# A graph kernel: scatters held at two points of each slot, record codes stored as pairs, six source masks by ScalarE, and the third layer norm in six parts

## The reference

```python
edge_index = stack([src, dst])                       # 400000 edges, dst sorted
h = maximum(_layernorm(x), 0)                        # x is 12500 x 48
x = x + (segment_sum(edge_weight[:, None] * h[dst], src, N) @ weight + bias)
h = maximum(_layernorm(x), 0)
x = x + ((1 + eps[0]) * h + segment_sum(maximum(h[src] + edge_attr_48, 0), dst, N))
h = maximum(_layernorm(x), 0)
x = x + L2(h)     # twice: symmetric-normalised sum over the edges and self loops
h = maximum(_layernorm(x), 0)
x = x + L3(h)     # the same once, in the other direction
return x
```

## Time and profile before

| | us |
|---|---|
| runs | 10912.69, 10917.33, 10930.52 |
| median | 10917.33 |
| profiled execution, its own time | 10818.04 |
| its span | 10816.2 |
| busy: PE, DVE, ACT, POOL | 6417.2, 4776.5, 3992.4, 4088.1 |

### The profile page before, as it was taken

The page is one execution under the profiler, slowest core; times in us unless marked ns, Lnnn a source line. Parts: engine busy times, 40 slices in busy tenths (PEclk is TensorE's granted clock), DMA queues, the critical chain, the costliest instruction groups (busy, mean ns, idle before and its releaser), DMA issues.

```text
span 10816.2 us, 266700 instructions
## 1 busy us (share of the span) xinstructions
PE 6417.2 (59%) x100278; PEld 5569.8 (51%) x100279; DVE 4776.5 (44%) x7168; ACT 3992.4 (37%) x6938; POOL 4088.1 (38%) x4193
## 2 busy tenths in 40 slices
PE   5444444444444444444444444445999979999999
PEld 4333333333333333333333333335888879999998
DVE  5444444444444444444444443448999940111000
ACT  3333333333333333333333333335888820000333
POOL 2444444444444444444444444443888820000000
PEclk6666666666666666666666666667999989999999
DMA  6444444444444444444444444445999978888998
GB/s 172 141 146 146 143 143 140 142 138 146 144 144 146 147 144 142 139 137 142 145 146 147 147 142 138 145 148 180 317 317 317 316 247 265 275 279 273 195 204 178
DMA packets 1738803, 1964.50 MB, mean 182 GB/s; under 512 B 897469, under 2 KB 1403119, under 8 KB 1737791
## 3 DMA queue, kind: packets, MB, share of 16 engines
q1 hardware_dynamic: 1337520, 1347.06, 43.2%
q10 hardware_dynamic: 300646, 448.79, 12.1%
q0 software_dynamic: 100000, 158.60, 4.7%
HBM read 1258.29 MB, written 618.65 MB: 174 GB/s over the span
## 4 chain that ended last, share of the span: by engine, by line
PE 38%; another core or an unknown queue 25%; issue 13%; DVE 8%; ACT 8%; ACTq 3%; DMA 2%; POOL 1%; SPq 1%; DVEq 1%; POOLq 0%
PE pG L2174 7%; PE pT L2057 6%; ACT stg L2431 4%; PE pG L2013 3%; PE pT L2061 2%; PE pT L2174 2%; PE pG L2024 2%; PE pG L2226 2%; PE pR L2174 2%; PE pG L2022 2%; PE pG L2213 2%; DVE msum L1825 2%; ACT dfar L2398 1%; PE pG L2138 1%
## 5 line engine op out<-in xcount | busy, mean ns | idle before, releaser
L1359 POOL DMA_INDIRECT recB<-rec,qpos x3125 | 3046.9, 975 | 4294.4 <-issue 3403.0
L2057 PE MATMUL pT<-soh,doh 128*128 128x128 bf16 x10600 | 1771.6, 268 | 3412.7 <-ACT stg L2431 3032.7
L2431 ACT CAST stg<-pT 128x512 fp8e4<-128x512 f32 x2650 | 1499.7, 585 | 3989.4 <-remote 3050.9
L2057 PEld LDWEIGHTS pT<-soh,doh 128*128 128x128 bf16 x10600 | 1027.9, 117 | 3642.7 <-ACT stg L2431 3154.7
L1641 DVE TENSOR_TENSOR rec<-pG,wN 128x480 f32<-128x480 f32 x314 | 205.5, 654 | 2252.6 <-PE pG L2013 2241.9
L1628 DVE TENSOR_TENSOR soh<-smd,pG 128x1280 bf16<-128x1280 bf16 x530 | 432.5, 816 | 1314.4 <-remote 866.9
L2061 PE MATMUL pT<-car,qidb 128*128 128x256 fp8e4 x2597 | 925.1, 356 | 0.0
L2138 PE MATMUL pG<-mpl,doh 128*128 128x144 bf16 x10388 | 764.3, 227 | 34.0 <-POOL mpl L1380 25.0
L1628 DVE TENSOR_TENSOR doh<-dm,pG 128x2560 bf16<-128x2560 bf16 x530 | 782.7, 1477 | 1.5 <-ACT dm L2509 0.9
L1628 DVE TENSOR_TENSOR doh<-smd,pG 128x2560 bf16<-128x2560 bf16 x530 | 783.1, 1478 | 0.0
L2138 PEld LDWEIGHTS pG<-mpl,doh 128*128 128x128 bf16 x10388 | 666.0, 96 | 63.6 <-POOL mpl L1380 49.1
(11 more groups left out here) (266 smaller groups left out, 14329.2 us busy)
## 6 DMA issues: line engine op xcount, KB each, us to landing
recB<-zt ACTq DMA_DIRECT2D x102, 2425.5 KB
brec<-recB SPq DMA_DIRECT2D x477, 495.0 KB
erec<-recB SPq DMA_DIRECT2D x477, 495.0 KB, 5.5
cl<-cA SPq DMA_DIRECT2D x80, 2560.0 KB, 10.8
cA<-stg ACTq DMA_DIRECT2D x530, 320.0 KB
cl<-cA SPq DMA_DIRECT2D x40, 2720.0 KB, 11.1
drow<-dlD SPq DMA_DIRECT2D x157, 640.0 KB, 5.8
srowB<-srD SPq DMA_DIRECT2D x265, 320.0 KB, 5.8
```

The lines of the kernel that those rows point to most:

```text
L1359: p.indirect_dma_start(recF, bass.IndirectOffsetOnAxis(ap=qpos[:, s, c:c + 1], axis=0), rec[:, s, c, :], None).then_inc(s_sc[s], 16)
L2057: ins = t.matmul(bank[:, h * 256 + b * 128:h * 256 + b * 128 + 128], doh[:, o, 2 * e + b, h * 128:(h + 1) * 128], soh[:, o, 2 * e + b, :], ...
L2431: a.copy(stg[:, o, :, e * 256:(e + 1) * 256], B8[6 + (g * 5 + e) % 2][:, :].rearrange("p (h x) -> p h x", h=2), saturate=False).then_inc(e ...
```

## The change

Five things change.

1. In `scatter`, POOL waits ahead of the scatters 7 and 14 of each slot until `e_ca` has reached the count of `PACE`, from chunk 2 on. Chunk 1 is now written out ahead of the loop, without these waits. The counts start from the second group that the slot sums (`SUMMED[s][1]`), five to a group.
2. The two codes are written into the records as bfloat16 pairs (`meta`, and −1 in the empty records). `places` and `codes` go; DVE's `one_hots` reads the loaded records. The load of `brec` waits for ACT's evictions too.
3. In the third stage ACT makes the masks of six groups (`BY_ACT`), DVE those of four.
4. The layer norm between the stages goes in the six parts of `UN`. SP loads all of `part`, from 49 stored chunks on, its parts between the first loads of `cl`; PE waits for each part.
5. At the start, the first prefill is issued ahead of the table's zeros, and the large load of x after the second prefill.

A tenth check of the input's form joins the nine. The diff, cut to its core:

```diff
@@ -1245,9 +1262,13 @@
+        BY_ACT = [1, 3, 4, 6, 8, 9]
+        BY_DVE = [g for g in range(JG) if g not in BY_ACT]
@@ -1344,25 +1365,36 @@
-            def scatter(K, s, first=False):
+            PACE = {0: {7: 9, 14: 14}, 1: {7: 9, 14: 14}, 2: {7: 14, 14: 15}}
+
+            def paced(K, s, c):
+
+                back, g = SUMMED[s][1]
+                hold(p, e_ca, ((K - back) * JG + g) * 5 + PACE[s][c])
+
...
                 if first:
-                    p.wait_ge(q_ld[2], 64)
+                    p.wait_ge(s_p0, 32)
...
                 for c in range(15 if first else 0, SB):
+                    if pace and c in PACE[s]:
+                        paced(K, s, c)
                     p.indirect_dma_start(recF, bass.IndirectOffsetOnAxis(ap=qpos[:, s, c:c + 1], axis=0),
                                          rec[:, s, c, :], None).then_inc(s_sc[s], 16)
 
             scatter(0, 2, True)
-            with p.Fori(1, NK) as K:
+            for s in range(3):
+                scatter(1, s)
+            with p.Fori(2, NK) as K:
                 for s in range(3):
-                    scatter(K, s)
+                    scatter(K, s, pace=True)
@@ -1672,10 +1705,9 @@
-                v.wait_ge(e_sm, c + 1)
+                v.wait_ge(l_b[r], K * 64 + (g // 5 * 32 + 32))
                 reached(v, e_ca, c * 5 - 5)
-                one_hots(soh[:, o, :, :], smd[:, r, :, 0, :], GB, 128, ioA)
-                v.wait_ge(l_b[r], K * 64 + (g // 5 * 32 + 32))
+                one_hots(soh[:, o, :, :], brec_u[:, r, :, 97, :], GB, 128, ioA)
@@ -1683,7 +1715,7 @@
-                one_hots(doh[:, o, :, :], smd[:, r, :, 1, :], GB, 256, ioA)
+                one_hots(doh[:, o, :, :], brec_u[:, r, :, 98, :], GB, 256, ioA)
@@ -1794,16 +1826,16 @@
-                    if g % 2 == 0:
+                    if g in BY_DVE:
...
-                    v.wait_ge(m_dm, c + 1)
+                    v.wait_ge(k_e[r], K * 32 + (g // 5 * 16 + 16))
                     reached(v, m_sc, c - 4)
-                    one_hots(doh5[:, r, :, :], dm5[:, r, :, :], GB, 256, ioB).then_inc(m_do, 1)
+                    one_hots(doh5[:, r, :, :], erec_u[:, r, :, 98, :], GB, 256, ioB).then_inc(m_do, 1)
@@ -1828,17 +1860,52 @@
-                collect(NK - 1, (NK - 1) % 2)
-                nch.mark("free")
-                for b, (lo, hi) in enumerate(HALF):
-                    v.wait_ge(s_half[b], 32)
+
+                def centred(u):
...
-                    centre(2, b, qx3, qst)
-                summed(2, SQ2, hs_)
-                for b in range(2):
-                    scaled(2, b, SQ2, True)
-                    rests(2, b, xpc, qh3, qh_u, scr, scr_u)
+                    nch(v.tensor_reduce(qst[:, 0, lo:hi], qx3[:, lo:hi, :], AX.X, ALU.add))
...
+                centred(0)
+                collect(NK - 1, (NK - 1) % 2)
+                varied(0)
+                normed(0)
+                centred(1)
+                varied(1)
...
+                for u in range(2, len(UN)):
+                    varied(u)
+                    if u + 1 < len(UN):
+                        centred(u + 1)
+                    normed(u)
@@ -2154,6 +2221,7 @@
                 gather1(NK - 1, JG - 1, (NK - 1) % 2)
+                t.wait_ge(m_ev, NK)
...
-                                for b in ({0: 0, 2: 1}[u],) if u in (0, 2) else ():
-                                    t.wait_ge(e_qn, qn[f"pcs2{b}"])
-                                    t.wait_ge(t_sq, SQ2 + 6 + 2 * b)
+                                t.wait_ge(e_qn, qn[f"pcs2{u}"])
+                                t.wait_ge(t_sq, sqn[f"lo{u}"])
@@ -2386,8 +2453,10 @@
-                a.copy(rec[:, s, :, 97], srcl[:, bass.ds(ncol(K, s), SB)])
-                a.copy(rec[:, s, :, 98], dlK[:, bass.ds(ncol(K, s), SB)]).then_inc(e_me, 1)
+                a.copy(rec_u[:, s, :, 97, :],
+                       srcl[:, bass.ds(ncol(K, s), SB)].unsqueeze(2).to_broadcast([128, SB, 2]))
+                a.copy(rec_u[:, s, :, 98, :],
+                       dlK[:, bass.ds(ncol(K, s), SB)].unsqueeze(2).to_broadcast([128, SB, 2])).then_inc(e_me, 1)
@@ -2401,26 +2470,11 @@
-            def places(K, g):
-                c = K * JG + g
-                r = g % 5
-                a.wait_ge(l_b[r], K * 64 + (g // 5 * 32 + 32))
-                reached(a, e_pl, c - 4)
-                a.copy(smd[:, r, :, :, :],
-                       brec[:, r, :, 97:99].unsqueeze(3).to_broadcast([128, GB, 2, 2])).then_inc(e_sm, 1)
...
-                a.copy(smK[:, g * GB:(g + 1) * GB], smd[:, g % 5, :, 0, 0])
+                a.wait_ge(l_b[g % 5], K * 64 + (g // 5 * 32 + 32))
+                a.copy(smK[:, g * GB:(g + 1) * GB], brec_u[:, g % 5, :, 97, 1])
@@ -2501,25 +2554,18 @@
-                def codes(K, g):
-                    c = K * JG + g
-                    r = g % 5
-                    a.wait_ge(k_e[r], K * 32 + (g // 5 * 16 + 16))
-                    reached(a, m_do, c - 4)
-                    a.copy(dm5[:, r, :, :], erec[:, r, :, 98:99].to_broadcast([128, GB, 2])).then_inc(m_dm, 1)
-
@@ -2527,28 +2573,45 @@
-                    if not (known and K == NK - 1 and g >= JG - 2):
-                        codes(K + (g + 2) // JG, (g + 2) % JG)
...
-                    n = g + (2 if o else 3)
-                    if not (known and K == NK - 1 and n >= JG):
-                        (none_away if o else distances)(K + n // JG, n % JG)
...
+                    for n, part_ in ((g + 2, none_away), (g + 3, distances)):
+                        if n % JG in BY_ACT and not (known and K == NK - 1 and n >= JG):
+                            part_(K + n // JG, n % JG)
...
-                a.wait_ge(e_qn, qn["free"])
-                hold(a, s_nw, NK * 16)
-                for b, (lo, hi) in enumerate(HALF):
@@ -2597,13 +2660,12 @@
-            sp.dma_start(qx3[:, 8:NB - 1, :], x[8 * 128:(NB - 1) * 128, :].rearrange("(j p) d -> p j d", p=128)
-                         ).then_inc(q_ld[3], 16)
             sp.wait_ge(e_q, qm["c0"])
-            sp.dma_start(qx3[0:N - (NB - 1) * 128, NB - 1, :], x[(NB - 1) * 128:N, :]).then_inc(q_ld[3], 16)
             sp.dma_start(hT[NP:NPX, :].rearrange("(p r) c -> p (r c)", p=128),
                          zz[:, 0:144].bitcast(BF16)).then_inc(q_st, 16)
             sp.wait_ge(e_q, qm["zt"])
+            for h in range(2):
+                prefill(sp, 0, h, s_p0)
             sp.wait_ge(q_st, 32)
@@ -2635,6 +2697,7 @@
                 held(sp, e_ag, c - 4)
+                held(sp, e_cv, (c - 5) * 5 + 1)
@@ -2651,14 +2714,14 @@
-            sp.wait_ge(q_ld[2], 32)
-            for h in range(2):
-                prefill(sp, 0, h, q_ld[2])
             sp.wait_ge(e_q, qm["codes"])
             load_ea(0, 2)
+            sp.wait_ge(q_ld[0], 48)
             for h in range(2):
                 prefill(sp, 1, h)
-            sp.wait_ge(q_ld[0], 48)
+            sp.dma_start(qx3[:, 8:NB - 1, :], x[8 * 128:(NB - 1) * 128, :].rearrange("(j p) d -> p j d", p=128)
+                         ).then_inc(q_ld[3], 16)
+            sp.dma_start(qx3[0:N - (NB - 1) * 128, NB - 1, :], x[(NB - 1) * 128:N, :]).then_inc(q_ld[3], 16)
@@ -2713,10 +2775,10 @@
-                        hold(sp, *((m_sT, K * 5 + (g - 3) // 2) if g % 2 else (m_sU, K * 5 + (g - 4) // 2)))
-                    tab, w = (srD8, 64) if g % 2 else (srD, 128)
+                        hold(sp, *rowed(K - (g < 5), (g - 5) % JG))
+                    tab, w = (srD8, 64) if g in BY_ACT else (srD, 128)
@@ -2735,26 +2797,44 @@
-                steps(sp, step)
-                store_chunk(NK - 1)
-                sp.wait_ge(s_nw, NK * 16)
-                sp.wait_ge(e_qn, qn["free"])
-                for b, (lo, hi) in enumerate(HALF):
-                    sp.dma_start(qh3[:, lo:hi, :], part[lo * 128:hi * 128, :].rearrange("(j p) c -> p j c", p=128)
...
+                def load_part(u):
+
+                    lo, hi = UP[u]
+                    if u >= 2:
+                        hold(sp, s_half[u % 2], u // 2 * 32)
+                    sp.dma_start(qh3[:, lo:hi, :], part[lo * 128:hi * 128, :].rearrange("(j p) c -> p j c", p=128)
+                                 ).then_inc(s_half[u % 2], 16)
+                    sp.dma_start(scr[:, lo:hi, :], part[NPX + lo * 128:NPX + hi * 128, :].rearrange("(j p) c -> p j c", p=128)
+                                 ).then_inc(s_half[u % 2], 16)
+
+                steps(sp, step)
+                hold(sp, s_nw, KL * 16)
+                load_part(0)
+                load_cA(0, 0, (0,))
+                load_part(1)
+                hold(sp, m_ad, NK * JG)
+                load_cA(0, 0, (1,))
+                load_part(2)
+                store_chunk(NK - 1)
+                load_cA(0, 0, (2,))
+                load_part(3)
+                load_part(4)
+                hold(sp, s_nw, NK * 16)
+                load_part(5)
+                load_cA(0, 0, (3, 4, 5))
```

(32 more changed lines are left out.)

122 lines of the change are left out of this document (80 added, 42 removed).

## The result

The changed kernel took 10292.74 us (median of 4 runs, 10284.63 to 10311.25) against 10923.19 before; the ratio is 0.9426, with a 95% interval of 0.9409 to 0.9443. The range held the time, but the forecast (10710) did not: the kernel gained three times what I had said.

A forecast was written before the change was run, and what follows sets the result against it. First half bound by waits, third stage by DVE; −102 (waits) − 30 (codes) − 33 (third stage) − 40 (layer) = −205 of the profiled 10818.0, so 10613, by the median's 1.0092 10710 us; range 10200 to 10930, forecast's own 10584 to 10822.

The forecast's parts named there:

- What bounds the first half: First half: bound by waits; a burst of scatters holds back PE's signals, which clear some 3 us after it.
- The count of the waits that bind: POOL's scatters: slot 0 stops at 7 and 14, slot 1 at 14, slot 2 at 7; 4 waits a chunk.
- The price of a pause: First half: each binding wait costs 3.05 us less one step, 2.16 to 2.57 us; 8.6 to 10.3 a chunk.
- rival C: First half: a short burst clears sooner, in 1.07 us; 10291 us by the median, chance 0.17.
- What passes in the fresh runs: First half: 13.6 steps a chunk leave the free stretch; with the pauses' cost, −2.0 us a chunk, −102 us.
- Codes as pairs: First half: ACT's casts `smd` and `dm` go, so DVE's `soh` waits less; −30 us taken, at most 211.3.
- Third stage: Third stage: DVE makes one source mask fewer a chunk, −38 us; −33 taken because DMA is close.
- The bound named next: Third stage: DMA at 22.8 us a chunk stands next behind DVE at 23.0.
- The layer in parts: Between third and dense stage: PE waits for one part at a time; −40 us, bounds −20 and −49.
- Start: Start of the kernel: the x load leaves SP's queue ahead of `drow`; 0 us, bounds −15 and +10.
- Rivals D and E: First half: PE's clock stays low, 11293 us, chance 0.13; scatters wait for DVE's one-hots, 11015 us, chance 0.03.

The follow-up runs named there:

- before_paced: The kernel before with the two waits a slot alone, codes, third stage, layer and start unchanged; 10322.49 us, ratio 0.9471.
- act_five: The changed kernel with five source masks a chunk by ACT and five by DVE, as before the change; 10277.64 us, ratio 0.9434 to before.
- no_pace_act64: The changed kernel without its two waits a slot, with 64 one-element copies on ACT ahead of its chunk loop; 10949.0 us, ratio 1.0048 to before.

## Why the prediction was wrong

1. **What bounds the first half: right as far as the traces go.** Beside a burst PE's work passes in the first part of the run and comes back some 3 us behind the last scatter. That the burst itself holds its signals back is the reading that fits all eight kernels; no run shows the mechanism. The waits were the largest term, as forecast, and they alone give what the first half gained.

2. **The count of the waits that bind: wrong.** "Slot 1 at 14 alone, slot 2 at 7 alone, so 4 waits a chunk". The counts start from the second group of the slot, which the text on the change says; in slots 1 and 2 I took them from the first, five steps too low. In the trace of before the steps done from that base are 7.1, 6.2 and 7.0 at scatter 7 of the three slots and 8.4, 7.2 and 9.0 at scatter 14, all under the thresholds. Slot 1 stops at 7 too (7.0 us on the mean) and slot 2's pause at 7 is 13.8 us. Five waits bind.

3. **The price of a pause: right in size.** 4 × (3.05 less one step) was 8.6 to 10.3 us a chunk. The trace shows 10.5 more in the first 3 us behind the runs (19.5 against 9.0). That is for three more gaps of over 3 us (six, where before had three) and one of 1.7 us: five pauses came, but the gap ahead of slot 2 vanished and that ahead of slot 1 nearly did. Nor does a run of 7 clear as soon as rival C had it (1.07 us). PE begins 8.0 matmul records in the first 3 us behind such a run and 12.8 in the fourth, against 7.4 and 8.8 behind the bursts of 20 before. So the mechanism of C, whose time (10291) came out, is not what happened.

4. **What passes in the fresh runs, and what it is worth: the step that failed.** I gave "13.6 steps a chunk that leave the free stretch" at 0.74 to 0.89 us, 10 to 12 us, and took −2.0 a chunk for the waits. No step left it. Counted by evictions, as in the prediction, 17.4 steps a chunk began beside the scatters before the change and 9.3 after, so eight moved into the pauses and gaps. What moved the other way is the work that stands behind the steps in PE's program. A pause lets PE finish the slot's steps; next come the gathers for the following slot and, behind the first group of its steps, its last ranks and a count. Gathers and counts now run beside the scatters with 130 matmuls a chunk, where it was 9; the others came behind the burst. In PE's order they stand ahead of the rank that gives the next burst's last places, so the next burst can start sooner: the gap ahead of slot 0 fell from 24.2 to 11.7 us, those ahead of slots 1 and 2 from 19 and 20 us to 1.7 and 0.3, against 42.7 us of pauses. Beyond the first 3 us behind the runs the free time fell by 17.5 us (54.1 to 36.6), where I had 10 to 12. With the 10.5 us of point 3 and 1.8 us less of the scatters' own time (75.8 to 74.0) that is the measured −8.9 a chunk within rounding, −9.7 with the waits alone. I took every fresh run to bring the same work as the first, without asking what PE has to do next when a pause ends. Behind the last chunk another 18 us went that I hadn't counted (127.4 to 109.4); `before_paced` has them too (108.9), so they are the waits'. That fewer steps are left over there is my reading, not shown.

5. **Codes as pairs: no gain.** I took −30 us, as one cast less on the path. Without the waits the chunk is 12.2 us longer than before's, of which 8.4 is the loading of ACT's code: there the sign was wrong. With the waits it is 0.8 us longer than in `before_paced`, but 0.2 in `act_five` (129.4), whose first half is the same, so little more than nothing is shown. That an edit moves a loop in an engine's program had no term at all.

6. **Third stage: mis-sized.** −33 taken, −10 measured in the trace. DVE's own work fell as forecast, to 1079.91 of 1100 us, or 23.0 of a chunk's 23.42. The bound named next (22.8 us by DMA) wasn't reached; waits between PE, ACT and DVE came first, PE's for ACT's mask above all.

7. **The layer in parts: right,** at its bound. −49 against −40; PE waits 6.07 us. The dense stage is 5.5 us longer; I had set 10 to 30 for the loads behind the parts, and no run shows that they are the cause.

8. **Start: right** (−4 against 0). The first scatter comes 10.5 us earlier (68.26, not 78.79), and 6.7 of it are lost again by chunk 2.

9. **Rivals D and E** did not happen. The clock rose from 0.61 to 0.66 in a chunk; in the rest of the free time it is 0.71 where it was 0.75, still between the two levels. Scatters beside DVE's one-hots take 968 ns on the mean and those beside no work of DVE 957; before it was 1006 and 957. By the Trainium skill's rule (SBUF — State Buffer, "SBUF: two separate sides") some of VectorE's operations would have blocked GpSimd until they ended; the trace shows 11 ns, and not the 1.48 us of a one-hot.

That the waits pay was right; by what, and how much, was wrong. That 10292 lay near rival C's 10291 is chance. The forecast's own range, 10584 to 10822, should by its terms read 10586 to 10826, which changes nothing. What stays open is why one wait at 7 gives as much as two. Its gathers run beside the scatters too (143.3 a chunk), but the counts of edges do not. Open as well is whether the break as such would do, or PE must have finished its steps in it.

## What to carry to other kernels

Where one engine's work stalls beside another's long bursts of DMA starts (here 25 us), a break in the burst can pay even though it costs a few microseconds to recover: look up in the other engine's program what stands next when the break ends, for that is what passes in the opening, and ask whether it lies on the path to the next burst. Read a threshold's base in the code before counting which waits bind. An edit can cost by where it puts a loop in an engine's program: compare the packets of the instruction queues and the idle time behind "issue" before and after, and test it with a shift that does nothing.

## What the runs showed of the hardware that was not expected

- While POOL issues indirect DMAs 1.26 us apart, PE's work goes on for the first 4.4 us of a run (38 to 43 records a run in all kernels) and nearly stops after (before the change 36 records in the 20.9 us that are left of a burst; by kernel this rest takes 36 to 118 records a chunk, the most with one wait at 7). Behind the last scatter it comes back after some 3 us, for runs of 7 (8.0 records in the first 3 us, 12.8 in the fourth) as for bursts of 20 before (7.4 and 8.8); in `no_pace_act64` after 4 (1.3, 1.3, then 10.1 in the fifth).
- The same loop on ACT, 20 instructions a chunk shorter than before, was loaded anew in each chunk (five loads of 8 KB); shifted by 64 instructions it was not. Where no pause covered it, this cost 8.4 us a chunk (151.1 to 142.7), where pauses at scatter 7 did, nothing (129.6 and 129.6).
